# Attention in two layers: the row maxima of the next pair ahead of the scores in TensorE's order

## What is computed

```python
q = (x @ Wq).reshape(b, t, 2 * H, HD).transpose(0, 2, 1, 3) * scaling
k = (x @ Wk).reshape(b, t, 2 * H, HD).transpose(0, 2, 1, 3)
v = (x @ Wv).reshape(b, t, H, 2 * HD).transpose(0, 2, 1, 3)
scores = jnp.einsum('bhqd,bhkd->bhqk', q, k)
aw = jax.nn.softmax((scores + causal).astype(jnp.float32), axis=-1)
aw = aw.reshape(b, H, 2, t, t)
aw = aw[:, :, 0] - lam * aw[:, :, 1]
attn = jnp.einsum('bhqk,bhkd->bhqd', aw, v)
```

## Time and profile before

| | |
|---|---|
| median of 3 runs | 3548.26 us (3547.71 to 3548.54) |
| the profiled execution | 3550.99 us |
| its span | 3549.0 us |
| mean granted TensorE clock | 0.977 of full speed |
| busy over the span | PE 95%, DVE 75%, ACT 59%, POOL 25% |
| the attention stage | 166 to 1220 us |

### The profile page before, as it was taken

The page is one execution under the profiler, slowest core; times in us unless marked ns, Lnnn a source line. Parts: engine busy times, 40 slices in busy tenths (PEclk is TensorE's granted clock), DMA queues, the critical chain, the costliest instruction groups (busy, mean ns, idle before and its releaser), DMA issues. The chain is left out here.

```text
span 3549.0 us, 58273 instructions
## 1 busy us (share of the span) xinstructions
PE 3370.3 (95%) x20672; PEld 2378.6 (67%) x20672; DVE 2677.5 (75%) x5224; ACT 2110.0 (59%) x3378; POOL 880.6 (25%) x818
## 2 busy tenths in 40 slices
PE   9899999999999888977999999999999999969998
PEld 7644444444444477765777777777777777758886
DVE  3577777777777484575999999999998999964444
ACT  3156666666667633434777777777777777743332
POOL 0012212222222300002344434443444444420000
PEclk9999999999999998988999999999999999989999
DMA  7333433433432211237666766677667766640100
GB/s 243 84 79 90 113 86 100 110 88 100 108 90 86 101 39 35 86 113 243 235 225 230 245 233 227 231 254 243 228 227 231 247 228 231 216 141 27 36 12 24
DMA packets 263840, 529.34 MB, mean 149 GB/s; under 512 B 32256, under 2 KB 54912, under 8 KB 260480
## 3 DMA queue, kind: packets, MB, share of 16 engines
q1 hardware_dynamic: 263552, 525.62, 46.7%
HBM read 429.55 MB, written 95.42 MB: 148 GB/s over the span
## 5 line engine op out<-in xcount | busy, mean ns | idle before, releaser
L628 ACT ACTIVATE probs<-prob_scores 128x1024 f32<-128x1024 f32 (+3 forms) x640 | 572.8, 897 | 382.2 <-PE prob_scores L560 374.4
L583 PE MATMUL times_v<-probs,VS 128*64 128x256 f32 (+2 forms) x4608 | 613.5, 382 | 17.5 <-ACT outT L662 12.7
L684 DVE TENSOR_REDUCE part_max<-ring 128x1 f32<-128x512 f32 x720 | 463.0, 686 | 112.4 <-PE ring L552 110.7
L49 PE MATMUL sc_pip<-sc_xh,sc_wl 128*128 128x512 f32 x1024 | 455.7, 445 | 22.3 <-DMA sc_xl<-x_low 15.4
L583 PEld LDWEIGHTS times_v<-probs,VS 128*64 128x64 f32 x4608 | 279.8, 136 | 256.8 <-issue 161.8
L51 PE MATMUL sc_pip<-sc_xh,sc_wh 128*128 128x512 f32 x1024 | 405.2, 396 | 0.0
L50 PE MATMUL sc_pip<-sc_xl,sc_wh 128*128 128x512 f32 x1024 | 403.9, 394 | 0.0
L1754 POOL TENSOR_TENSOR sc_xdd<-sc_xdt,sc_small 128x512 f32<-128x512 f32 x128 | 245.6, 1919 | 581.5 <-DVE sc_xdt L1965 581.5
L1890 ACT ACTIVATE sc_M<-sc_later,sc_small 128x128 f32<-128x128 f32 x1024 | 311.8, 390 | 0.0
L560 PE MATMUL prob_scores<-QS,KS 50*128 50x512 f32 (+3 forms) x1280 | 298.8, 464 | 4.0 <-ACT probs L628 2.1
L1956 DVE SCALAR_TENSOR_TENSOR sc_ca<-sc_xr,sc_chan,sc_ca 128x512 f32<-128x512 f32 x384 | 290.9, 758 | 13.6
(11 more groups left out here) (376 smaller groups left out, 7163.6 us busy)
## 6 DMA issues: line engine op xcount, KB each, us to landing
sc_wh<-scan_W_high SPq DMA_DIRECT2D x256, 256.0 KB, 2.8
sc_wl<-scan_W_low SPq DMA_DIRECT2D x256, 256.0 KB, 3.4
sc_later<-scan_acum SPq DMA_DIRECT2D x128, 512.0 KB, 4.9
sc_ce<-scan_expa SPq DMA_DIRECT2D x128, 512.0 KB, 5.2
sc_woh<-scan_Wo_high SPq DMA_DIRECT2D x128, 256.0 KB, 4.1
sc_wol<-scan_Wo_low SPq DMA_DIRECT2D x128, 256.0 KB, 4.8
w_raw<-in_Wg SPq DMA_DIRECT2D x64, 256.0 KB, 2.9
scan_W_high<-w_hi SPq DMA_DIRECT2D x64, 256.0 KB, 2.0
```

The source lines that it names most:

```text
L49: pe.matmul(out, ll, rh, start=start, stop=False)
L583: mm = pe.matmul(po[MV * s:MV * (s + 1), CHUNK - w + n * h:CHUNK - w + (n + 1) * h], VS[p % 2][:, j, :], PT[u % NPT][:, s, n * h:(n + 1) * ...
L628: act.activation(PT[u % NPT][:, :, 0:w], pb[u % 2][:, :, 0:w], ACT.Exp).then_inc(exped, 1)
L684: dve.tensor_reduce(to, slot(n)[:, 0:w], AX.X, ALU.max).then_inc(emptied, 1)
```

## The change

In each step the loop that issues `max_scores` stands ahead of the block that waits for `exped` and issues `scores`; before, it stood behind it. VectorE's and ScalarE's programs, the order of the ring's slots and all sizes stay.

```diff
                     for u in range(NU):
                         n = p * NU + u
                         to = p + (u + LEAD) // NU
+                        for q, t in step_tiles(p, u):
+                            max_scores(q, t)
                         if to < PAIRS:
                             if u + LEAD == NU:
                                 pe.wait_ge(max_in[to % NQK], rows(to))
 
                             pe.wait_ge(exped, n + 1)
                             scores(to % NQK, (u + LEAD) % NU)
-                        for q, t in step_tiles(p, u):
-                            max_scores(q, t)
                         if u == TURN_AT and p + 1 < PAIRS:
                             turn_maxima(p + 1)
                         times_v(p, u)
```

## The result

The changed kernel takes 3581.4 us (median of 4 runs, 3577.6 to 3584.5) against 3548.0 us before; the ratio is 1.0096, with a 95% interval of 1.0078 to 1.0113. It is slower, by 33 us; 3576 was forecast, with 3561 to 3588 as the range. Its profiled execution is the fastest of the four: 3577.63 us, span 3575.6 us.

A forecast was written before the change was run, and what follows sets the result against it. TensorE was taken to bound the attention; four copy waits of 0.23 us and four ring waits of 0.24 us per pair, over 14 pairs plus 1.5 us for pair 0, gave 27.8 us more: 3576 us, range 3561 to 3588.

The forecast's parts named there:

- TensorE sets the pace: Attention pairs: TensorE is busy 64.1 of 65.4 us, so the change is worth what it does to TensorE's order.
- an ordinary step costs the same in both orders: Steps away from chunk ends: still 1.68 us, zero change, with 0.01 us per step either way as the bound.
- The first term, the copy: Each of four chunk ends: later scores delay exp, ScalarE's PSUM copy and the next times-V matmuls by 0.23 us.
- The second term, the ring: Three steps behind each chunk end: scores now wait behind row maxima for the ring slot, 0.24 us more.
- The weakest case: Second chunk's ring wait: VectorE's first reduction ends 0.21 us after the step began; still 0.24 us more.
- Rival (e): Later exp meets later GpSimd and VectorE work in a new 0.5 us collision once per pair: 3583 us; chance 0.07.
- The sum: Attention: 1.88 us per pair over 14 pairs, 26.3 us, plus 1.5 us for pair 0, 27.8 us in all.
- rival (a): Chunk ends: only one of the two waits, on the copy or the ring slot, grows; 14 us, 3562; chance 0.12.
- Rival (d): Clock falls to 1.2 GHz for one step after each of eight longer waits per pair: 140 us, 3716; chance 0.02.
- (b): Steps with row maxima: these fill the scores' real wait for exp, 0.10 us each, 56 us less, 3492; chance 0.04.
- (c): Chunk ends: order is indifferent, waits set by times-V matmuls and output turning alone; 3548 within 7 us; chance 0.05.

The follow-up runs named there:

- the pair of experiments with nine units: Changed kernel with scores first again at units 1, 2, 3, 6, 11, 14, 23, 26, 39: 3552.4 us; mirror, row maxima first only there: 3584.0 us.
- the experiment with the filled waits: Changed kernel with score matmuls issued twice more at units 0, 4, 12, 24 and once more at units 2, 26, inside TensorE's waits: median 3581.5 us.

## Why the prediction was right

*TensorE sets the pace, and an ordinary step costs the same in both orders*: right, 1.68 us before and after, and the pair of experiments with nine units shows it from both sides.

*The first term, the copy*: right. It was to be 0.23 us at each of four ends; measured from T to T it is 0.24, 0.24, 0.24 and, at the third chunk, 0.27. The old order at the ends takes it away, less what L706 loses there.

*The second term, the ring*: right. 0.24 us at each of four places was said; 0.23, 0.24 and 0.24 in units 6, 14 and 26. The weakest case, unit 14, was worked out from where VectorE's first reduction ended, and came out so.

*At unit 2 the size was off*: 0.53 where 0.24 was said. This is the term that was mis-sized, and most of the difference between the pair's 67.3 us forecast and 67.65 measured (0.29 of 0.37 us; 14 x 0.29 = 4.1 us). L714's delay is 0.25 of the 0.29, and the old order at unit 1 takes it away. I had checked for a collision of VectorE with GpSimd at the third chunk, found that both sides move together, and stopped there. Rival (e) named a new collision and gave it 0.5 us at an unnamed place and a chance of 0.07; it came, at half that price, at the pair's own end. The earlier trace rows show the mechanism already; what was missing was to ask it of every combine, with the mask L482 as well as with L489.

*The sum*: 27.8 us was forecast for the attention, and 31.2 measured in the profile. The pairs 1 to 13 took 30.5 us more (1.1 of it the one fall of the clock), pair 14 1.9 more, pair 15 0.5 less and pair 0 0.7 less. For pair 0 I had put 1.5 us more. That was right, and hidden by the clock: at the stage's start it stood at 0.50 for 13.6 us in the first profile of the kernel before and for 6.8 in that of the changed kernel. The changed kernel's second profile has 13.6 us too, and there pair 0 takes 77.8 us against 76.4, 1.5 more. That the first profile's sum comes so close to the forecast's is thus in part luck: the excess at unit 2 and the quicker start offset each other. (The range's lower end, named as that of rival (a), stands at 3561; (a) itself is 3562.)

*Rival (d), the clock*: there is a little in it. The granted clock did fall to 0.50 within the stage, once for 3.4 us and a loss of 1.1 us in the changed kernel's first profile, twice in its second, five times in the kernel with the old order at the ends and twice in the one with the new order at nine units; never between the start and the end of the stage in the two profiles of the kernel before. It was priced as if it followed every wait, and given 0.02; as a rule for every wait it is wrong, as a rare event it is worth 1 to 3 us. The Trainium skill ("TensorE: Matmul & The Clock Gate", section "A second HAM failure mode: psum-queue depth-cycling") has the clock swing at short idle times between groups of matmuls. The traces agree in part: no wait of TensorE in the pairs 1 to 14 of any kernel here was longer than 1.1 us and the clock fell behind some, but through most of them it stayed at 1.00. That the added waits cause these falls is likely, from where they lie: nine of the ten follow, within a step or two, a place where a distance from T to T, or two in a row, is 0.5 us longer than before (unit 2, or the third chunk's end with the new order at nine units), and no kernel without such a place showed one. It is not shown: the experiment with the filled waits did not settle it.

*Rivals (a), (b) and (c)*: out. Both terms go one by one; the 115 us booked as S waiting for exp were nobody's wait, for the R that now stands first in the step takes the same 0.10 us there.

## What to carry to other kernels

Moving a group of instructions ahead within a step of constant length costs nothing where every consumer has slack; look for the few steps where another engine stands idle waiting for the group that is moved back, and for waits under which it used to run: each cost 0.24 us here, the 0.34 us of the group that now stands ahead less the 0.10 us of weight load that moved with it, however small the busy share that it concerns. Then walk through each pair of engines that can hold each other up, at every place where one of the two moves against the other. Where a copy that frees a buffer stands behind a long operation in an in-order queue, look at moving the copy ahead: by itself it made a pair 0.59 us shorter here (65.39 to 64.80), and the order R, T, S on top of it 0.53 more.

## What the runs showed of the hardware

Two of VectorE's small operations between SBUF tiles are held until a GpSimd operation that began before them has ended: L706 (4 elements per partition) took 0.23 us alone and 0.67 to 1.09 us beside L489, L714 0.29 alone, 0.54 beside the mask L482 and 0.86 to 1.11 beside L489. L706 ended 0.02 to 0.03 us after L489, L714 0.13 to 0.16 us after GpSimd's operation. L707 and L710, which read PSUM, were 0.28 us throughout. The Trainium skill has this in "SBUF — State Buffer", section "Who interferes with whom": the port pair that the two share is an exclusive lock, taken by VectorE for an operation with two SBUF inputs, as L714 is, or in a two-port mode, and the one that comes second is fully blocked. The trace agrees, with the numbers above; whether L706, which has one tensor as input, ran in a two-port mode it does not show. What I had not expected is how far it reaches: shifts of 0.24 us between engines moved the collision from one instruction to the other and made differences of 0.24 to 0.75 us per pair in most of the kernels here.

A granted clock of 0.50 nearly doubles TensorE's streams: at such a place T took 1.97 us for 8 matmuls where it takes 1.08, while ScalarE's exp beside it kept its 1.02 us, and the pair lost 0.8 to 2.6 us. Which pairs it met differed between two executions of the same kernel, except for pair 6. Most of what differs between executions of one kernel, here up to 9 us behind the attention and 2 us at its start, goes with the time at 0.50.
